# B's score rows replicated by DMA through DRAM, the gate of B and C made on GpSimd, new orders on all engines

## The reference, cut to what matters

```python
# x: (32, 256, 256) float32, adj: (32, 256, 256) int32
def _L0_gnn_ref(h, adj, W, a):                       # layer A: one head
    Wh = jnp.matmul(h, W)
    e = Wh@a1 [:, :, None] + Wh@a2 [:, None, :]      # row score + column score
    e = leaky_relu(e, 0.2); e = where(adj == 0, MASK_VAL, e)
    return elu(softmax(e, axis=2) @ Wh)

def _L1_gnn_ref(adj, x, W1, ..., W2, ...):           # two GAT layers on one mask
    mask = (adj > 0) | eye
    h = elu(gat_layer(x, mask, W1, ..., concat=True))    # layer B: 4 heads of 128
    return gat_layer(h, mask, W2, ..., concat=False)     # layer C: one head of 256

x = layernorm(x + _L0_gnn_ref(x, adj, ...))
x = layernorm(x + _L1_gnn_ref(adj, x, ...))
```

## Time and profile before

| | before |
|---|---|
| median of 3 runs | 663.95 us |
| the profiled execution's own time | 664.63 us |
| its span (first to last instruction) | 662.9 us |
| PE busy | 637.5 us, 96% |
| DVE busy | 596.6 us, 90% |
| ACT busy | 473.9 us, 71% |
| POOL busy | 441.4 us, 67% |
| mean granted clock of TensorE | 0.988 |
| busy share of the 16 DMA engines, main queue | 20.4% |

### The profile page before, as it was taken

One profiled execution on the slowest core, in us unless ns is written; L12 is line 12 of the kernel. 1 busy time (PEld: TensorE's weight loads), 2 busy tenths in 40 slices (PEclk: granted clock), 3 DMA queues, 4 the chain that ended last, 5 costly groups with the idle time before them and its releaser, 6 DMA issues. The chain is left out here.

```text
span 662.9 us, 17540 instructions
## 1 busy us (share of the span) xinstructions
PE 637.5 (96%) x4166; PEld 570.7 (86%) x4166; DVE 596.6 (90%) x2369; ACT 473.9 (71%) x1220; POOL 441.4 (67%) x810
## 2 busy tenths in 40 slices
PE   7789999999999999999999999999999999999885
PEld 6468889998988999999899999998999999989774
DVE  3988999999999999999999999999999999998774
ACT  2367777777777877777777777777877777777671
POOL 0346677777767767677677767777777677666753
PEclk9699999999999999999999999999999999999999
DMA  6511022012222211222222022222211222210000
GB/s 217 164 48 58 9 81 71 31 61 81 81 82 80 80 42 43 81 81 81 81 81 67 32 65 81 82 81 81 81 40 43 80 81 82 82 45 20 18 17 32
DMA packets 46214, 45.42 MB, mean 69 GB/s; under 512 B 2721, under 2 KB 45729, under 8 KB 46114
## 3 DMA queue, kind: packets, MB, share of 16 engines
q1 hardware_dynamic: 45392, 43.26, 20.4%
q10 hardware_dynamic: 722, 1.05, 0.5%
HBM read 35.92 MB, written 8.39 MB: 67 GB/s over the span
## 5 line engine op out<-in xcount | busy, mean ns | idle before, releaser
L390 POOL TENSOR_SCALAR probB<-probB,rdenB 128x256 f32<-128x256 f32 x256 | 119.5, 479 | 64.1 <-DVE rdenB L991 63.3
L576 ACT ACTIVATE probB<-probB,shiftB 128x256 f32<-128x256 f32 x256 | 127.0, 498 | 36.4 <-DVE shiftB L960 33.8
L1583 PE MATMUL PS<-probTB,VB 128*128 128x256 f32 x512 | 127.6, 381 | 0.7 <-ACT probTB L595 0.6
L401 POOL TENSOR_TENSOR inlC<-hidT,inhC 128x512 fp32r<-128x512 f32 x64 | 81.7, 1278 | 52.9 <-ACT inhC L640 52.9
L974 DVE SCALAR_TENSOR_TENSOR probB<-PS,VB,gatedB 128x256 f32<-128x256 f32 x256 | 111.4, 476 | 1.4 <-issue 0.4
L1583 PEld LDWEIGHTS PS<-probTB,VB 128*128 128x128 f32 x512 | 89.6, 191 | 10.7 <-ACT probTB L595 1.2
L932 DVE CUSTOM_DVE_ANT_0 gatedB<-PS,gate_bc 128x256 f32<-128x256 f32 x256 | 93.5, 417 | 4.7 <-PE PS L1553 2.1
L595 ACT ACTIVATE probTB<-PS 128x512 f32<-128x512 f32 x128 | 74.6, 587 | 16.2 <-PE PS L1564 15.8
L1537 PE MATMUL PS<-WhB,inhB 128*128 128x260 f32 x256 | 81.2, 317 | 3.1 <-DVE inlB L1005 3.1
L1564 PE MATMUL PS<-ident,probB 128*128 128x128 f32 x512 | 77.2, 274 | 2.3 <-POOL probB L390 2.1
L1537 PE MATMUL PS<-WhC,inhC 128*128 128x258 f32 x256 | 76.5, 299 | 0.5 <-issue 0.4
(11 more groups left out here) (117 smaller groups left out, 1642.4 us busy)
## 6 DMA issues: line engine op xcount, KB each, us to landing
xTin<-in_x_t_dram SPq DMA_DIRECT2D x32, 256.0 KB, 3.0
adj_in<-in_adj_dram SPq DMA_DIRECT2D x32, 256.0 KB, 3.2
adjT_in<-in_adj_t_dram SPq DMA_DIRECT2D x32, 256.0 KB, 4.2
xres<-in_x_dram SPq DMA_DIRECT2D x32, 256.0 KB, 4.0
out_dram<-res SPq DMA_DIRECT2D x31, 256.0 KB, 2.1
WC<-in_L_gnn_W_dram SPq DMA_DIRECT2D x1, 512.0 KB, 8.6
WB<-in_L_gnn_W_dram SPq DMA_DIRECT2D x2, 256.0 KB, 7.4
attA<-in_L_gnn_a_dram ACTq DMA_DIRECT2D x1, 256.0 KB, 4.1
```

The costliest lines, as they stand in the source:

```text
L390: last = pool.tensor_scalar(B.prob[h][:, k, :], B.prob[h][:, k, :], B.rden[:, k, h:h + 1], 1.0, ALU.mult, ALU.mult)
L401: pool.tensor_tensor(C.inl[:, s, :], hidT[:, s, :], C.inh[:, s, :].bitcast(F32), ALU.subtract)\
L576: last = nc.scalar.activation(L.prob[h][:, k, :], L.prob[h][:, k, :], ACT.Exp, bias=L.shift[:, k, h:h + 1], accum_out=den[:, k, h:h + 1] i ...
L1583: last = nc.tensor.matmul(PS[b][:, o:o + N], B.V[:, k, h, 2:B.F + 2], B.probT[h][:, k, :], start=(k == 0), stop=(k == NT - 1))
```

## The change

1. **Score rows of B.** The two `spread(B, ...)` of a turn are gone from PE. In their place SP issues, for each group, two DMAs that write column 0 of V for one head each to a DRAM tensor of 2 x 512 floats (element by element, 256 elements of 4 bytes), waits for them, and issues one DMA that reads the line of 512 floats back to all 128 partitions of an SBUF tile `score` (256 KB written). `maxima` and `logit` of B read `score` where they read a PSUM bank before; those of A and C are as they were.
2. **Gate of B and C.** `make_gate_b` stands in POOL's program and no longer in DVE's, with the same operation and the same tiles.
3. **Buffers.** Two for B's V, three for each `score` group, four for `gate_bc` and `x1b`.
4. **Vectors.** The attention vectors and biases come as one row on one partition in one DMA, and PE spreads them over the partitions in the fill (`spread_vectors`, 4 matmuls of 512 columns); 5 broadcast DMAs are gone.
5. **Orders.** `fill`, `body` and `drain` of all engines are written in a new order; the oldest batch of a turn has lag 6, the repeated turns are again 25.

```diff
-            L.V = sb("V" + n, [P, NT, L.H, L.F + (2 if L is B else 3)])
+            L.NV = 2 if L is B else 1
+            L.V = [sb(f"V{n}{i}", [P, NT, L.H, L.F + (2 if L is B else 3)]) for i in range(L.NV)]
...
+        NR = 3
+        score = [[sb(f"score{i}{g}", [P, 2 * N]) for g in range(NG)] for i in range(NR)]
+        line = nc.dram_tensor("score_lines", [NG, 2 * N], F32, kind="Internal").ap()
...
+            def write_scores(g, t):
+                if active(t):
+                    for tile in range(NT):
+                        sp.wait_ge(B.s_v[tile][g], t.this())
+                    if t.later:
+                        sp.wait_ge(s_score[g], t.last(DMA))
+                    for h in range(2):
+                        sp.dma_start(line[g, h * N:(h + 1) * N].rearrange("(k p) -> p k", p=P),
+                                     B.V[t.at % B.NV][:, :, 2 * g + h, 0],
+                                     allow_slow_non_contiguous=True).then_inc(s_line[g], DMA)
+
+            def replicate_scores(g, t):
+                if active(t):
+                    sp.wait_ge(s_line[g], t.this(2 * DMA))
+                    if t.at >= NR:
+                        for s in B.s_logit[2 * g:2 * g + 2]:
+                            sp.wait_ge(s, t.this() - NR)
+                    sp.dma_start(score[t.at % NR][g][:, :], line[g].partition_broadcast(P))\
+                        .then_inc(s_score[g], DMA)
...
             def body(i):
                 load_xT(t0)
+                load_residual(t0)
                 load_adj(t0)
-                load_residual(t1)
+                write_scores(0, t3)
+                replicate_scores(0, t3)
+                write_scores(1, t2)
                 load_adjT(t1)
-                store(t5)
+                replicate_scores(1, t2)
+                store(t6)
...
+            def make_gate_b(t):                      # on POOL, gone from DVE
+                if active(t):
+                    pool.wait_ge(s_adjT[t.at % 2], t.loaded())
+                    if t.at >= 4:
+                        for s in B.s_max + C.s_max:
+                            pool.wait_ge(s, t.this() - 4)
+                    pool.tensor_scalar(gate_bc[t.at % 4][:, :, :], adjT_in[t.at % 2][:, :, :], 0, -BIG, ALU.is_le,
+                                            ALU.mult).then_inc(s_gB, 1)
...
+            def scores(L, h, b, t):
+                src = score[t.at % NR][h // 2] if L is B else PS[b]
+                return src[:, (h % 2) * N:(h % 2 + 1) * N]
...
             def maxima(L, h, b, t):
-                    dve.wait_ge(L.s_spread[h // 2], t.this())
+                    if L is B:
+                        dve.wait_ge(s_score[h // 2], t.this(DMA))
+                    else:
+                        dve.wait_ge(L.s_spread[0], t.this())
...
-                            out=L.gated[h][:, k, :], in0=PS[b][:, (h % 2) * N:(h % 2 + 1) * N],
+                            out=L.gated[h][:, k, :], in0=scores(L, h, b, t),
...
-                            out=L.prob[h][:, k, :], in0=PS[b][:, (h % 2) * N:(h % 2 + 1) * N],
-                            scalar=L.V[:, k, h, 1:2], in1=L.gated[h][:, k, :], op0=ALU.max, op1=ALU.add)
+                            out=L.prob[h][:, k, :], in0=scores(L, h, b, t),
+                            scalar=L.V[t.at % L.NV][:, k, h, 1:2], in1=L.gated[h][:, k, :], op0=ALU.max, op1=ALU.add)
...
+            def spread_vectors(L, j, b):
+                take_bank(b, [], Turn(0))
+                held[b] = [(L.s_wab, 2 * L.KT * L.H)]
+                pe.wait_ge(s_rows, DMA)
+                o = ROW[L][j]
+                nc.tensor.matmul(PS[b][:, :], ones[0:1, :], rows[:, o:o + 512], start=True, stop=True).then_inc(L.s_att, 1)
```

More of the change, by code:

```diff
@@ L190, in iterations @@
         def iterations(body):
-            for i in range(6, NB + 5 - 6):
+            for i in range(6, NB + 6 - 7):
                 body(Turn(i))
@@ L1135, in fill @@
+                logit(A, 0, 2, b2)
+                stats(A, b1)
+                values_b(0, 0, 1, b0)
+                meanvar(A, b1)
+                make_gate_a(b3)
+                values_b(1, 0, 4, b0)
+                inverse_sum(A, 0, 7, b2)
+                inverse_sum(A, 1, 4, b2)
+                maxima(B, 3, None, b0)
+                maxima(B, 2, None, b0)
+                low_b(5, b1)
+                logit(B, 2, None, b0)
                 top(B, 1, b0)
-                logit(B, 2, 7, b0)
+                elu_first(b2)
@@ new lines, in fill @@
+                stats(A, b2)
+                top(A, 0, b3)
+                inverse_sum_head(3, b0)
+                inverse_sum_head(2, b0)
+                shift(A, 0, b3)
+                logit(A, 0, 6, b3)
+                maxima(B, 0, None, b0)
+                meanvar(A, b2)
+                values_b(1, 0, 1, b1)
+                values_b(0, 0, 3, b1)
+                maxima(B, 1, None, b0)
+                logit(B, 0, None, b0)
+                logit(B, 1, None, b0)
+                inverse_sum(A, 0, 1, b3)
@@ L1240, in fill @@
[L1240 to L1252 removed]
+                values_b(0, 0, 5, b2)
@@ new lines, in drain @@
+                elu_first(e2)
+                logit(B, 2, None, e4)
+                maxima(A, 0, 6, e1)
+                inverse_sum(C, 0, 0, e7)
+                inverse_sum_head(3, e4)
+                stats(A, e2)
+                logit(A, 0, 6, e1)
+                top(A, 0, e1)
+                inverse_sum_head(0, e5)
+                shift(A, 0, e1)
+                inverse_sum_head(2, e4)
+                values_b(1, 1, 1, e3)
+                inverse_sum(C, 1, 7, e7)
+                meanvar(A, e2)
@@ new lines, in drain @@
+                inverse_sum_head(1, e5)
+                norm_last(0, 0, e7)
+                elu(1, 4, e5)
+                values_b(0, 1, 6, e3)
+                norm_last(1, 7, e7)
+                maxima(B, 1, None, e4)
+                stats(C, e7)
+                meanvar(C, e7)
+                maxima(B, 0, None, e4)
+                maxima(C, 0, 0, e6)
+                logit(C, 0, 0, e6)
+                top(C, 0, e6)
+                top(B, 0, e4)
+                shift(C, 0, e6)
+                elu(0, 1, e5)
@@ new lines, in drain @@
+                inverse_sum_head(3, e3)
+                values_b(1, 1, 7, e2)
+                meanvar(A, e1)
+                inverse_sum_head(2, e3)
+                maxima(B, 0, None, e3)
+                elu(1, 5, e4)
+                maxima(B, 1, None, e3)
+                logit(B, 1, None, e3)
+                top(B, 0, e3)
+                logit(B, 0, None, e3)
+                maxima(C, 0, 3, e5)
+                shift(B, 0, e3)
+                logit(C, 0, 3, e5)
+                values_b(1, 0, 7, e2)
```

1618 lines of the change are left out of this document (777 added, 841 removed).

## The result

| | before | after |
|---|---|---|
| median | 664.51 us (663.73 to 665.21, 4 runs) | 874.46 us (866.4 to 882.31, 4 runs) |
| ratio, 95% interval | | 1.312 (1.303 to 1.321) |
| profiled execution, span | 664.63, 662.9 us | 882.31, 880.6 us |
| PE, DVE, ACT, POOL busy | 96, 90, 71, 67% | 78, 71, 55, 62% |
| mean granted clock | 0.988 | 0.901 |

The change makes the kernel 31% slower. The forecast was slower, 725 us, within 650 to 790; the time is 84 us above the upper end.

A forecast was written before the change was run, and what follows sets the result against it. PE bounded the kernel at 19.2 us a turn, DVE 1.0 behind. Afterwards DVE would need 17.8 + 3.0 + 0.3 = 21.1 us; 1.9 more times 32 is 61, and 664.6 + 61 - 0.7 = 725 us, range 650 to 790.

The forecast's parts named there:

- PE's work without the spread: PE's turn without B's two transpose groups: 19.2 less 0.87, so 18.3 us.
- The way through DRAM: SP's score write, wait and read back: 7.4 us, up to 12, covered by DVE's other work, so put at 0.
- The port wait: B's sixteen two-SBUF-input DVE instructions wait for POOL at the shared port: 3.0 us a turn, ends 1.5 and 5.3; chance 0.64.
- POOL's instruction stops the first that meets it: Port wait on DVE if each POOL instruction holds back only the first B instruction meeting it: 3.9 us a turn.
- I expect 0.6: Sign in the profile after: B's maxima on DVE with a mean well over 0.42 us, about 0.6.
- The sum without the failed step: DVE's turn of 17.8 + 3.0 + 0.3 = 21.1 us, giving 725 us, with the DRAM path at 0.
- Gate on POOL: B and C's gate moved from DVE to POOL: 0.95 us there, within 0.5 to 1.3, covered by the turn.
- SP's queue is the bound: Rival: loads late behind the store on SP, or late scores, leave DVE idle 1 to 2 us a turn: 677 us; chance 0.12.
- PE stays the bound: Rival: POOL and DVE get by each other, turn 18.3 us and 636 us, or 650 with waits of 0.7; chance 0.20.
- no difference: Rival: DVE waits of 1.0 to 1.2 us a turn give back PE's gain: 660 to 667 us; chance 0.04.

The follow-up runs named there:

- e12: Changed kernel with 64 B between the written elements in DRAM, replications reading x instead of the line: 710.05 us, ratio 1.067.
- e5: Changed kernel with 512 B between the written elements in DRAM, replications reading x instead of the line: 718.73 us, ratio 1.077.
- e6: Changed kernel with its dense element writes kept and waited for, but replications reading x instead of the line: 893.05 us, ratio 1.344.
- e2: Kernel before, with B's maxima and logit reading a constant SBUF row instead of the PSUM bank, PE's spread still done: 762.02 us, ratio 1.147.
- e1: Changed kernel without the element writes to DRAM and their waits, replications reading x: 710.48 us, ratio 1.072.
- e10: Changed kernel with each write taking 256 numbers in a row from one partition, one 1 KB packet instead of 256 of 4 bytes: 710.84 us, ratio 1.070.
- e3: Kernel before, with only make_gate_b moved from DVE to POOL: 669.35 us, ratio 1.007.
- e11: Changed kernel with each write after the first batch taking 32 of the 256 elements, dense in DRAM: 737.89 us, ratio 1.110.

## Why the prediction was wrong

**PE's work without the spread: right.** In e12 it is 182.37 of 200 us in a turn of 20.5, 18.7 us against 18.3 forecast.

**The step that failed: "The way through DRAM. ... So I put it at 0, with 2 us a turn as upper end."** It was the largest term. I took the element write from the nearest row, the store's 2.1 us, because no row had packets of 4 bytes, and summed 7.4 us for the path, up to 12. It is 10.5 us from the write's issue to the next issue, queueing behind the loads included, and 16.1 from values to `maxima` (406.36 to 422.44). Worse than the size was how I used it: I compared it with 10 to 12 us of other work in DVE's order and took the comparison for one-sided. But the path closes a ring (values, write, replicate, `maxima`, ... values of the next batch), and SP walks it twice a turn, in order, with the waits in between. The right sum was on SP's own queue: 2 x (10.5 + 0.4) + 2.2 us of store and loads = 24.0. With my own upper figure, 12 us of path less some 4 of replication, it would have been 2 x 8.4 + 2.2 = 19, below the forecast turn of 21.1; with 10.5 it is the bound. So the size decides, and a price bounded only by rows of another form deserved a wide upper end and a rival of its own. The Trainium skill warned against just this form (page "DMA: Bandwidth & Descriptors", section "Rules for kernel authors"), and I cited it and gave it nothing. e5, e6 and e12 add to it that the number of such elements isn't what costs here: 256 of them land in 1.9 us if they go 64 B apart.

**The port wait: right in size, too wide in kind.** Forecast 3.0 us a turn. Measured in e12: 8 x (587 - 419) + 8 x (659 - 476) = 2.8; in e2 3.5. The picture of "POOL's instruction stops the first that meets it" is in e12's trace, for `low_c`:

```profile
400.24 1.46 POOL L462 TENSOR_TENSOR inlC<-hidT,inhC 128x512 fp32r<-128x512 f32 x1 [0.38 <-ACT inhC L709]
400.50 1.48 DVE L999 CUSTOM_DVE_ANT_0 gatedB<-score,gate_bc 128x256 f32<-128x256 f32 x1
401.78 1.98 POOL L390 TENSOR_SCALAR gate_bc<-adjT_in 128x512 bf16<-128x512 int32 x1
401.99 0.74 DVE L999 CUSTOM_DVE_ANT_0 gatedB<-score,gate_bc 128x256 f32<-128x256 f32 x1
402.65 0.42 DVE L999 CUSTOM_DVE_ANT_0 gatedB<-score,gate_bc 128x256 f32<-128x256 f32 x1
```

Over all 256 the median is 416 ns and the maximum 1,503 in e1: a minority waits for a whole instruction, and a median would hide it. In the changed kernel itself gatedB's mean is just 442 ns (probB's is 647), since in a turn of 25.5 us the two meet less often, as I read it; "I expect 0.6" failed there and held (0.59) once the write was out.

```profile
L999 DVE CUSTOM_DVE_ANT_0 gatedB<-score,gate_bc 128x256 f32<-128x256 f32 x256 | 103.7, 442 | 128.7 <-issue 93.1 <-DMA score<-score_lines 34.4
```

**The sum without the failed step: right.** Forecast 21.1 us a turn and 725; e1, e10 and e12 have 20.5 and 710 to 711.

**Gate on POOL: the cost was too low, the conclusion held.** 1.95 us, above my end of 1.3, but alone it is worth 0.7% (e3).

**Rivals.** "SP's queue is the bound" named the right engine with chance 0.12 and the wrong size: 677, worked out from the store's wait, with late scores in half a sentence at the same 677; the sign I had given for it, DVE idle before `gate_a` or `gatedB` with a DMA named, is what appeared. "PE stays the bound" and "no difference" are out.

**What stays open.** Why dense 4-byte writes land so late: about half of the wait passes with nothing left for the DMA engines to do, and 64 B between elements is enough to end it, but what is shared below 64 B, and why two writes of 256 cost no more than one while 32 cost a third, no run here tells. How much of the 10.5 us is queueing behind the loads was not split by a run either. How the granted clock (0.90 in the window, PE with idle gaps) and the slower landings of the other DMAs add to the 164 us was not split.

## What to carry to other kernels

When a value goes through DRAM between two steps of a pipeline, draw the ring that it closes and add up its landings on the one queue that waits for them; work beside it covers it only if the whole ring is shorter than the turn. If no row of the trace has the packet form (4-byte elements to neighbouring addresses), its price is unknown upward: measure it by itself first, as one replaced DMA does in e10 or e12. And for an operand moved from PSUM to SBUF in a two-input VectorE instruction, count the time that it overlaps GpSimd's instructions, those with two input tiles above all; here the forecast was 3.0 us and 2.8 were measured.

## What the runs showed of the hardware

- Writes of 256 4-byte elements to adjacent addresses in DRAM, two at a time: 10.4 us to landing (e11's first batch). 64 B apart: 1.9 us (e12); 512 B apart: 1.7 us (e5). 32 adjacent ones: 3.3 us (e11). In the dense form 5.1 us (median, e6) pass between the last 4-byte packet and the next issue, while a packet takes 9 ns as in e12. 1 KB in one piece: the next DMA was issued 1.4 us after the write's issue, wait included.
- In the kernel with the dense writes, other transfers of 256 KB land later: the store 5.1 us (2.2 in e12), adj_in 5.6 (3.7), xTin 4.7 (2.9). There SP issues them in one burst behind a replication, so the writes needn't be the cause; no run separates the two.
- An int32 128x512 comparison to bf16 takes 1.95 us on POOL and 0.40 on DVE, yet a DVE instruction with two SBUF inputs often ran at full speed beside it (56 of the 83 of B that started inside it in e12). Beside a POOL instruction with two input tiles none did (0 of 68).
